# A two-stage attention kernel for 16 sequences: second buffer for x, whole transposes of the input, linear-attention sums kept in one PSUM bank, setup inside the main block, and a new order table

## The reference, cut to what matters

```python
# linear attention, 16 heads of 8 columns, causal
q, k, v = heads(x @ Wq.T), heads(x @ Wk.T), heads(x @ Wv.T)
q, k = rope(q, k); q, k = elu(q) + 1, elu(k) + 1
KV_t = sum_{s<=t} k_s outer v_s ;  K_t = sum_{s<=t} k_s
y_t = (q_t @ KV_t) / max(q_t . K_t, 1e-6) ;  out = y @ Wo.T

# twice: local attention (8 heads of 64, window 64) and gated feed-forward
h = shift_token(x)              # right half of the columns moved down one row
q, k, v = split(h @ wqkv); q = l2norm(q) * qs; k = l2norm(k) * ksc; rotary_xpos(q, k)
x = x + local_attention(q, k, v) @ wo
h = layernorm(shift_token(x)) * lg + lb
a, g = split(h @ w1 + b1); x = x + (a * gelu(g)) @ w2 + b2
```

## Time and profile before

| | |
|---|---|
| median of 3 runs | 1835.49 us (1835.01 to 1836.9) |
| profiled execution, its own time | 1839.22 us |
| its span, first to last instruction | 1836.7 us |
| PE busy | 1641.0 us, 89% of the span |
| ACT, DVE, POOL busy | 74%, 72%, 70% |
| mean granted clock of TensorE | 0.971 of full speed |

### The profile page before, as it was taken

The page is one execution under the profiler, slowest core; times in us unless marked ns, Lnnn a source line. Parts: engine busy times, 40 slices in busy tenths (PEclk is TensorE's granted clock), DMA queues, the critical chain, the costliest instruction groups (busy, mean ns, idle before and its releaser), DMA issues.

```text
span 1836.7 us, 51372 instructions
## 1 busy us (share of the span) xinstructions
PE 1641.0 (89%) x18212; PEld 1149.2 (63%) x18340; DVE 1329.3 (72%) x3471; ACT 1367.3 (74%) x4277; POOL 1285.8 (70%) x1715
## 2 busy tenths in 40 slices
PE   0677989999999999999999999999999999998875
PEld 0344666666667666666666666666667666666653
DVE  2465777877777787877778787777777787776552
ACT  1264768787887878798887878787787878788663
POOL 1263777777777887777777787777777887777562
PEclk9888999999999999999999999999999999999986
DMA  3000001011111011111111011111101011111001
GB/s 117 12 16 19 22 23 25 18 36 30 36 28 28 19 34 27 31 36 30 36 28 28 19 31 30 31 36 28 39 22 31 22 25 36 30 31 30 19 21 29
DMA packets 58135, 54.52 MB, mean 30 GB/s; under 512 B 7538, under 2 KB 42780, under 8 KB 57756
## 3 DMA queue, kind: packets, MB, share of 16 engines
q1 hardware_dynamic: 57884, 51.25, 11.0%
HBM read 13.48 MB, written 8.39 MB: 12 GB/s over the span
## 4 chain that ended last, share of the span: by engine, by line
PE 70%; ACT 12%; POOL 7%; issue 6%; DVE 3%; DMA 0%; POOLq 0%; ACTq 0%; DVEq 0%; SPq 0%
PE bank L732 10%; PE bank L787 7%; PE bank L759 7%; PE bank L798 5%; PE bank L744 5%; PE bank L771 5%; PE bank L838 4%; PE bank L827 4%; PE bank L679 4%; PE bank L695 3%; PE bank L753 2%; PE bank L719 2%; ACT probs L959 2%; ACT probs_t L853 2%; POOL qk_rows L1308 2%
## 5 line engine op out<-in xcount | busy, mean ns | idle before, releaser
L959 ACT ACTIVATE probs<-bank,s_low 128x128 f32<-128x128 f32 x1024 | 360.1, 384 | 60.7 <-DVE s_low L1171 60.6
L1308 POOL TENSOR_TENSOR qk_rows<-qk_rows,qk_tmp 128x512 f32<-128x512 f32 x256 | 328.2, 1282 | 16.6 <-DVE qk_tmp L1159 15.8
L1321 POOL TENSOR_TENSOR probs<-probs,s_rden 128x512 f32<-128x512 f32 x256 | 263.5, 1050 | 68.1 <-DVE s_rden L1180 68.1
L732 PE MATMUL bank<-wqkv_sb,h_cols 128*128 128x512 f16 x1152 | 281.2, 388 | 7.9 <-ACT probs_t L853 2.6
L1311 POOL TENSOR_TENSOR qk_rows<-qk_rows,qk_rnorm 128x512 f32<-128x512 f32 x256 | 268.7, 1050 | 20.1
L959 ACT ACTIVATION_READ_ACCUMULATOR probs<-bank,s_low 128x1 f32 x1024 | 229.0, 224 | 0.0
L1156 DVE TENSOR_TENSOR qk_rows<-bank,rope 128x512 f32<-128x512 f32 x256 | 174.4, 681 | 39.2 <-POOL qk_rows L1311 35.4
L1126 DVE TENSOR_TENSOR room<-bank,const 128x512 f32<-128x512 f32 x256 | 158.7, 683 | 57.8 <-PE bank L679 56.2
L732 PEld LDWEIGHTS bank<-wqkv_sb,h_cols 128*128 128x128 f16 x1152 | 108.2, 99 | 142.7 <-issue 22.7
L853 ACT ACTIVATE probs_t<-bank 128x512 f32<-128x512 f32 x256 | 140.9, 598 | 67.9 <-PE bank L771 65.2
L1142 DVE TENSOR_REDUCE qk_sum<-qk_sq 128x16 f32<-128x1024 f32 x128 | 155.1, 1212 | 46.2 <-ACT qk_sq L918 44.2
(11 more groups left out here) (154 smaller groups left out, 3650.6 us busy)
## 6 DMA issues: line engine op xcount, KB each, us to landing
v_even<-v_rows SPq DMA_DIRECT2D x224, 128.0 KB, 2.3
x_in<-in_L_attn_x SPq DMA_DIRECT2D x16, 256.0 KB, 3.2
kept_rows<-x_in SPq DMA_DIRECT2D x16, 256.0 KB, 2.3
x_back<-kept_rows SPq DMA_DIRECT2D x16, 256.0 KB, 3.0
out<-x_back SPq DMA_DIRECT2D x16, 256.0 KB, 2.4
room<-in_constants SPq DMA_DIRECT2D x1, 1024.0 KB
hidden<-in_L_ffn_wqkv SPq DMA_DIRECT2D x1, 768.0 KB
qk_rows<-in_L_ffn_wqkv SPq DMA_DIRECT2D x1, 768.0 KB
```

The lines of the kernel that those rows point to most:

```text
L732: mm = pe.matmul(to[:, :], h_cols[st.l][:, x_half, st.j * P:(st.j + 1) * P], wqkv_sb[:, st.l, w_half, w * INNER:(w + 1) * INNER], start=(n ...
L959: act.activation(probs[st.l][:, n, :], bank[b[half]][:, c * P:(c + 1) * P], ACT.Exp, bias=s_low[st.l][:, a, n:n + 1], accum_out=s_sum[st.l ...
L1308: pool.tensor_tensor(rows(w), rows(w), qk_tmp[l][:, w, :], ALU.add).then_inc(pool_qk.of(st), 1)
L1321: pool.tensor_tensor(probs[l][:, mine, :], probs[l][:, mine, :], s_rden[l][:, a, mine].unsqueeze(2).to_broadcast([P, PAIRS, P]), ALU.mult) ...
```

## The change

Six edits, all in one:

1. **Setup in the main block.** x of element 0 is loaded first, then the four linear weights and the small constants (`first_loaded`, 5 loads beside x), then the rest by layer (`loaded[l]`). The first element starts after the first group. The setup work of ACT and DVE is put between steps of element 0: `halve(0)`, `halve(1)`, `lower_weights(l)`, `turn_tables(l)`, `turn_masks`, and `qkv` and `rope` wait for `ready[l]`. Each engine raises its own start values (`start_signals`). The memsets are smaller and signal `zeroed`.
2. **Two buffers for x** (`x_in[:, st.n % 2]`): the load of n waits for the use of n-2. The normed attention rows go to `att_rows` (the memory of `y_cols`).
3. **`at`**: the two sums stay in one bank, `sums_bank[n]`, from tile 0 to tile 3. Each tile adds `anticausal` times the last tile's keys (which completes that tile's sum) and the last tile's key-value product, then the `causal` product: 4 products and transposes in tiles 1 to 3, where there were 4, 6 and 8. In exchange `at` of tile j waits until `den` of j-1 has read the bank, and the bank is in use from tile 0's `at` to tile 3's `den`.
4. **`as`** takes its four banks before its first product; `la_qexp` has one buffer in place of two.
5. **`h`**: four whole transposes. ACT and DVE each copy in two parts, the lower 64 rows one column further on.
6. **Order table**: `STARTS`, `TIMES` and `HOLD` have other values throughout.

```diff
-        x_in = sb("x_in", [P, NT, D])
+        x_in = sb("x_in", [P, 2, NT, D])
...
-        la_qexp = room[:, 0:1024].rearrange("p (a s q) -> p a s q", a=2, s=SLOTS)
+        la_qexp = room[:, 0:512].rearrange("p (s q) -> p s q", s=SLOTS)
...
-                    sp.wait_ge(*x_kept.at(st, back=1))
-                    sp.wait_ge(*act_ln["mid"].at(st, back=1))
-                    sp.dma_start(x_in[:, :, :], rows_of(x, st)).then_inc(x_loaded.of(st), 16)
+                    sp.wait_ge(*x_kept.at(st, back=2))
+                    sp.wait_ge(*act_ln["mid"].at(st, back=2))
+                    sp.dma_start(x_in[:, st.n % 2, :, :], rows_of(x, st)).then_inc(x_loaded.of(st), 16)
...
                     to, j = take(banks, 0), st.j
+                    if j == 0:
+                        take(banks, 1)
+                    sums = bank[sums_bank[st.n]]
+                    if j > 0:
+                        pe.wait_ge(*dve_aden.at(st.of("den", j - 1), 2))
+                        pe.matmul(sums[:, 0:P], cst("anticausal"), la_phi[:, j - 1, D:2 * D], start=False, stop=False,
+                                  skip_group_check=True)
+                        pe.wait_ge(*act_av.at(st.of("av", j - 1)))
+                        pe.matmul(sums[:, P:2 * P], la_phi[:, j - 1, D:2 * D], la_v[:, j - 1, :], start=False,
+                                  stop=True, skip_group_check=True)
                     pe.wait_ge(*dve_aphi.at(st))
-                    pe.matmul(to[:, 0:P], cst("causal"), la_phi[:, j, D:2 * D], start=True, stop=(j == 0),
+                    pe.matmul(sums[:, 0:P], cst("causal"), la_phi[:, j, D:2 * D], start=(j == 0), stop=True,
                               skip_group_check=True)
-                    for past in range(j):
-                        pe.matmul(to[:, 0:P], cst("ones"), la_phi[:, past, D:2 * D], start=False,
-                                  stop=(past == j - 1), skip_group_check=True)
-                    if j > 0:
-                        pe.wait_ge(*act_av.at(st.of("av", j - 1)))
-                    for past in range(j):
-                        pe.matmul(to[:, 3 * P:4 * P], la_phi[:, past, D:2 * D], la_v[:, past, :], start=False,
-                                  stop=(past == j - 1), skip_group_check=True)
                     pe.transpose(to[:, 2 * P:3 * P], la_phi[:, j, D:2 * D], ident).then_inc(pe_ak.of(st), 1)
...
-                    pe.matmul(to[DH:P, 0:1], ident[:, DH:P], cst("causal")[:, 0:1], start=True, stop=True)
                     for j in range(NT):
-                        n = min(P, T - 1 - j * P)
-                        pe.matmul(to[DH:P, j * P + 1:j * P + 1 + n], x_res[st.l][0:n, j, DH:D], ident[0:n, 0:n],
-                                  start=True, stop=True)
-                        mm = pe.transpose(to[0:DH, j * P:(j + 1) * P], x_res[st.l][:, j, 0:DH], ident)
+                        mm = pe.transpose(to[:, j * P:(j + 1) * P], x_res[st.l][:, j, :], ident)
                     mm.then_inc(pe_h.of(st), 1)
...
-                    copy(h_cols[st.l][:, 0, :], bank[b[0]][:, :]).then_inc(act_h.of(st), 1)
+                    copy(to[0:DH, 0, :], bank[b[0]][0:DH, :]).then_inc(act_h.of(st), 1)
+                    copy(to[DH:P, 0, 1:T], bank[b[0]][DH:P, 0:T - 1]).then_inc(act_h.of(st), 1)
...
-                    dve.tensor_tensor(h_cols[st.l][:, 1, :], bank[b[0]][:, :], h_cols[st.l][:, 0, :],
+                    dve.tensor_tensor(to[0:DH, 1, :], bank[b[0]][0:DH, :], to[0:DH, 0, :],
+                                      ALU.subtract).then_inc(dve_h.of(st), 1)
+                    dve.tensor_tensor(to[DH:P, 1, 1:T], bank[b[0]][DH:P, 0:T - 1], to[DH:P, 0, 1:T],
                                       ALU.subtract).then_inc(dve_h.of(st), 1)
...
+                    if st.name() == ("av", 0, NT - 1, 0):
+                        halve(0)
+                    if st.name() == ("ao", 0, 0, 0):
+                        halve(1)
...
+                    if st.name() == ("den", 0, 1, 0):
+                        lower_weights(0)
+                    if st.name() == ("mask", 0, 0, 0):
+                        turn_tables(0)
+                        turn_masks()
+                    if st.name() == ("mask", 0, 3, 0):
+                        lower_weights(1)
+                    if st.name() == ("ln_mid", 0, 0, 0):
+                        turn_tables(1)
```

More of the change, by code:

```diff
@@ L53, in _constants @@
     put("slot", (p[:, None] // LA_DH) % SLOTS == np.arange(SLOTS)[None, :])
-    put("ones", np.ones((P, P)))
+    put("anticausal", (p[:, None] > p[None, :]))
     half = LA_DH // 2
@@ L195 @@
+        "keep": [[27299]],
+        "bring": [[76501]],
+        "store": [[85711]],
+        "v_up": [[23386, 24669, 24845, 25009], [39583, 44097, 48321, 51619]],
+        "v_down": [[21942, 24668, 27905], [46883, 48063, 49037]],
     },
@@ L237, in banks_of @@
         banks[step.name()] = []
-        for u in range(count.get(step.kind, 0)):
-            b = min(range(BANKS), key=lambda b: (free[b], b))
+        for u in range(1 if step.kind == "at" and step.j > 0 else count.get(step.kind, 0)):
+            b = min(set(range(BANKS)) - set(banks[step.name()]), key=lambda b: (free[b], b))
             banks[step.name()].append(b)
@@ new lines, in build, with start_signals @@
+        ready = [ctx.enter_context(nc.semaphore(f"weights_ready_{l}")) for l in range(DEPTH)]
+        FIRST_LOADS = 5
+        LOADS = [1 + 1 + 1 + 1 + 1 + 1 + 6 + 2 + 2 + (1 if l == 0 else 0) for l in range(DEPTH)]
+        ZEROED = 17
+        READY = [3 + 2 + 4 * NT + (3 if l == 0 else 0) for l in range(DEPTH)]
+        def start_signals(engine, mine):
+            for sig in every:
+                if sig.name.split("_")[0] in mine:
+                    for sem in sig.sems:
+                        engine.sem_inc(sem, sig.start())
@@ L624, in _ @@
+                start_signals(sp, ("x", "out", "v", "sh"))
+                for at, (_, st) in enumerate(order["sync"]):
+                    if at > 0:
+                        run(st)
+                        continue
+                    sp.dma_start(x_in[:, 0, :, :], rows_of(x, st)).then_inc(x_loaded.of(st), 16)
+                    load_first()
+                    for l in range(DEPTH):
+                        load_layer(l)
+                    sp.wait_ge(zeroed, ZEROED)
                 sp.wait_ge(*out_stored.at(Step("store", 0, 0, B - 1)))
@@ L846, in _ @@
                 planned = plan()
+                start_signals(pe, ("pe",))
+                pe.wait_ge(first_loaded, 16 * FIRST_LOADS)
+                for n in range(4):
+                    mm = pe.transpose(bank[0][:, n * D:(n + 1) * D], la_rows[:, n * D:(n + 1) * D], ident)
+                mm.then_inc(turned, 1)
+                pe.wait_ge(la_ready, 2)
                 for _, st in order["tensor"]:
+                    if st.kind == "qkv" and st.n == 0 and st.j == 0:
+                        pe.wait_ge(ready[st.l], READY[st.l])
                     does[st.kind](st, planned[st.name()])
@@ L1010, in _, with halve @@
                 on_gelu = True
+                def halve(l):
+                    act.wait_ge(loaded[l], 16 * LOADS[l])
+                    for whole, halves in ((whole_wqkv[l], wqkv_sb[:, l, :, :]), (whole_w1[l], w1_sb[:, l, :, :])):
+                        act.activation(halves[:, 0, :], whole, ACT.Copy, scale=W_SCALE).then_inc(halved, 1)
+                start_signals(act, ("act",))
+                act.wait_ge(zeroed, ZEROED)
                 for _, st in order["scalar"]:
```

373 lines of the change are left out of this document (185 added, 188 removed), and 32 rows, old and new, of tables (HOLD, TIMES).

## The result

The changed kernel takes **1766.15 us** (median of 4 runs, 1765.96 to 1767.92) against 1835.66 us of the kernel before (1835.01 to 1836.9): a ratio of 0.9623, 95% interval 0.9606 to 0.9639. That is 3.8% faster where 4.9% was forecast, 21 us above the predicted 1745. The time lies 4 us outside the forecast's own range (1728 to 1762) and inside the range as the rival on ACT stretches it (to 1788). I had called it wrong in size from 7 us of idle time of PE per period on; there are 6.7.

A forecast was written before the change was run, and what follows sets the result against it. PE was taken as the bound, busy 99.7 of 104.0 us per period. Start 15, fill 234, twelve periods 1196 and drain 301 gave 1746 us of span, 1745 us of time; own range 1728 to 1762, stretched to 1724 and 1788.

The forecast's parts named there:

- the rival on ACT: ACT's added work holds PE up in the steady period: period between 101 and 104 us, 1773 us, up to 1796; chance 27%.
- The loads: Busy time per steady period: PE 94.4 us, ACT 88.9, DVE 84.1, POOL 80.3, with 95 table loads.
- The start: Time until PE's `yt` of element 0: 15 us (bounds 12 and 25), 28 us earlier than before.
- The drain: Last piece of the span: 6 us less PE work, part of the added table loads showing, 304.7 - 4 = 301 us.
- PE's idle time: PE's waits in a steady period: +1.9 us of new ones, -0.5 - 0.5 of old ones, +0.9 us on 4.3.
- `h` for ACT's copies: In layer 1, `h` on PE waits for ACT's two copies out of the `qkt` bank, some 0.75 us.
- the third bank of `qkv`: In layer 1, `qkv` on PE waits for a bank that `mask` of tile 1 on DVE reads, some 0.7 us.
- Edits at nothing: Edits priced at no time: four `as` banks at once, single `la_qexp`, start values raised on each engine.
- The premise under the sum: In the steady period a us off PE's work is worth a us, unless another engine comes near; PE's cut 5.3 us.
- the rival on the start: First loads share queues or setup falls on the path: 10 to 14 of 28 us lost, 1755 to 1765; chance 4%.
- Less idle time: PE's idle time per period falls to 3 us: period 97.4 to 98, 1720 to 1725 us; chance 8%.
- a slower kernel: `at` of tile 3 waits for `den` of tile 2 on DVE, stalling PE: at 8.5 us per period 1847 us; chance 3%.

The follow-up runs named there:

- `at` undone: The changed kernel with its `at` taken back, all past tiles summed anew by 6 more products per element on PE: 1779.39 us.
- `h` undone: The changed kernel with its `h` taken back, PE again shifting by products, ACT and DVE one step each instead of two: 1799.32 us.
- `h` alone: The kernel before, in its own order and setup, with only the whole transposes of `h` and the split copies on ACT and DVE: 1817.80 us.
- most of the change: The changed kernel with `at` taken back and the order tables of before (`STARTS`, `TIMES`, `HOLD`): 1810.94 us.
- a further cut of 1.1 us: The changed kernel with three instead of four products in each `wo` on PE, order kept, output differs: 1763.88 us.
- the two relu kernels: The changed kernel, order kept, with the third gelu of layer 1 as relu (64 loads): 1764.75 us; with all gelus as relus (2 loads): 1758.86 us.
- the kernel with the moved `guess`: The changed kernel with the layer-1 `guess` of tile 1 moved behind the third gelu in ACT's order, 64 table loads: 1815.79 us.

## Why the prediction was right, and where it was off

**The loads: right.** PE 94.8 us per period (94.4 forecast), ACT 88.8 (88.9), DVE 84.8 (84.1), POOL 79.9 (80.3); 95 table loads (47 + 47 + 1). `h` is followed by the next step after 0.43 us, from 956.47 to 956.90. A load costs ACT 1.28 us: in twelve periods it has 69 instructions and 87.8 us less without the loads (1064.89 and 977.11 us), 1.27 us for each. The drain of about 1.38 us that the Trainium skill gives beside the load (ScalarE: Activation LUTs, "What ACT_TABLE_LOAD costs") is not seen in this case's traces: ACT is idle for 0.8 us in all ahead of the 47 loads of L994, the last figure of their row above.

**The start: right.** `yt` of element 0 at 16.4 us (15 forecast), that of element 3 at 244.7 (249). The fill is 6 us shorter than I said. PE's work in it fell by 19 us (186.7 to 167.6) where I had counted 14, and DVE has 9 us more; what its setup, for which I added 3.5 us, costs the fill cannot be read apart from that.

**The drain: right**, 302.4 us (301), with luck in it: PE has 11 us less work there (256.2 to 245.4), where I had counted 6, and the drain is only 2.3 us shorter. The granted clock there is 0.94 instead of 0.91, for which the sum had no term; what it gives was not separated.

**PE's idle time: the term that failed.** I wrote "+1.9 of new waits and -0.5 - 0.5 of old ones: +0.9 us"; measured are +2.3. With PE's work, which fell by 4.9 us and not by 5.3 (`at` undone shows 1.0 of its 1.3, `h` undone 3.6 of its 4.0), the period is 1.75 us longer than forecast, 101.45 instead of 99.7. Twelve of them are 21 us, the size of the error; start and fill give 4.3 back, the drain takes 1.4, and 3 are in how the median stands to the span. Of its parts, `h` for ACT's copies was right (0.9 against 0.75) and the old waits shrank by more than I said (`yt` 0.9 to 0, the issue gaps 1.0 to 0.5); the third bank of `qkv` and the bank of `at` in tile 1 show no wait. What I lacked were `as` (1.3) and `pt` (1.2). For `as` the step was in the sentence "Edits at nothing: taking the four `as` banks at once". The cover that I named, masks done when PE arrives, is short by 0.4 us a time in the changed kernel (5.6 us in 13 waits). Another wait of `as`, 0.6 us a time, is for a bank that `exps` on ACT still reads, and in the order of before the rows name neither but `la_qk_cols` on ACT and `h_rows` on DVE: with four banks taken at once, the one that comes free last decides.

**The premise under the sum: wrong as it stood.** "A us off PE's work is worth a us per period as long as none of the other three comes near." The others were 6 to 15 us away and the gain was 2.7 of 4.9 us. In the order of before it is 1.1 of 3.2 with `h` alone, and 0.2 of 3.5 with most of the change. `at` undone gives 0.8 of 1.0, `h` undone 2.0 of 3.6, and a further cut of 1.1 us gives 0.2. In both orders the whole transposes of `h` bring back 1.6 to 2 us of waits for 3.2 to 3.6 us of work, which may be most of the growth of the idle time. My sum came near since the change brings an order remade for its code, worth 32 us against the order of before, and I had no term for that: that part is luck.

**The rivals.** ACT's additions reaching PE (27%, 1773 us): the time lies nearer to that than to the forecast, but the added loads are not the cause, as the two relu kernels show, and the added copies were not tested by themselves. That the stretched range holds the measured time is owed to this rival, whose main cause did not come about. In the rival on the start, "10 to 14 us" and "10 to 20" are two numbers for one loss; nothing rests on it. Less idle time (8%), a start that does not come earlier (4%) and a slower kernel (3%): none came. For the last, no row shows `at` waiting for `den` or `la_state`.

**Open.** What taking four `as` banks at once costs by itself, what the second copies and subtractions of `h` cost, what the setup in the main block and the second buffer for x are worth by themselves, and how much of the new order's 32 us is its bank table (`HOLD`) and how much the places of the steps (`TIMES`), was not tried.

## What to carry to other kernels

In a software pipeline with an order written out by hand, an engine that is busy 96% of a period need not be what sets it: take a little work from each engine in turn with the order kept, and see how much of each cut reaches the period. Compare periods at the same granted clock: one stretch at the lower level made a period 1.4 to 1.9 us longer here, more than the effect looked for. Price a cut as a range from nothing to the whole of it, with the lower end where the order is not remade, and give a remade order a term of its own. List every step that now takes several buffers at once as a wait of its own, also where the cover looks sufficient.

## What the runs showed of the hardware that I had not expected

A copy on half the partitions costs as much as on all. Groups of ACT and of DVE in one period of the changed kernel (busy, mean ns of one):

```profile
L823 ACT ACTIVATE probs_t<-bank 128x512 f32<-128x512 f32 x16 | 8.9, 601 | 4.2 <-PE bank L733 4.1
...
L823 ACT ACTIVATE h_cols<-bank 64x512 f16<-64x512 f32 (+1 forms) x4 | 2.4, 594 | 0.0
...
L1119 DVE TENSOR_TENSOR h_cols<-bank,h_cols 64x512 f16<-64x512 f32 x2 | 1.4, 678 | 0.8 <-ACT h_cols L823 0.8
```

The 594 ns for 64 partitions stand beside 601 for 128, and DVE's 678 beside 686 for the whole subtraction. For ACT I had left this open with a bound at half.

POOL's operation was not so flat: with 256 in place of 512 columns its division fell from 1051 to 613 ns, by 42% and not by half. And the sum of durations is not PE's time: dropping a quarter of `wo`'s products, 2.1 us by their group's mean, took 1.1 us off PE's busy time.

Waits of PE were followed by a lower clock. In the kernel with the moved `guess` each of the seven stretches at 1.2 GHz, 3.4 us long, starts within a us behind a wait of 1.7 us, which itself follows one of 0.6 us; the periods that hold one are 1.5 us longer on average than the other five. The same two waits stand in those five as well, and the clock behind them stays at 2.4 GHz, so they are not the whole condition.
